# Which engine makes the high parts of q and k, and when q and k are turned: three attention stages of a fused four-layer kernel on one core

## The chip, the core and the metric

One core of a Trainium2 chip runs the whole program. The metric is device microseconds of one execution. The kernel before has a median of 1841.68 us over 3 runs (1833.33 to 1843.39). Engine names as in the profile: PE is TensorE's matmul queue and PEld its weight loads, DVE is VectorE, ACT is ScalarE, POOL is GpSimd, SP is SyncE.

## The reference, cut to what matters

Eight sublayers are added one after another to x, 32 sequences of 128 tokens and 128 features. Three of them are attention with 16 heads of width 8:

```
x = x + L0_xattn(layernorm(x), ctx)         # "cross": biases, output projection
...
x = x + L2_xattn(layernorm(x), ctx, mask)   # "masked": no biases, no output projection
x = x + L2_ffn(layernorm(x))                # begins with causal self attention ("self"):
                                            # rotary q and k, 4 k/v heads, a tanh gate
# in each: softmax(q k^T / sqrt(8)) v, 16 heads
```

The other sublayers (routed experts, attention with one head, attention with 8 heads) aren't touched by the change.

## The kernel before

The function `attention16` writes the three stages, called "cross", "masked" and "self" in its argument `kind`. An item is one sequence (128 tokens on the 128 partitions); there are 32 items. Each engine runs a software pipeline written out by hand: at tick t (`unrolled`), `item(lag)` is item t - lag, and each engine's loop lists which step it does for which lag, in a fixed order. An engine does its list strictly in order, so an instruction that waits on a semaphore holds all that stands behind it on that engine. The tick length is set by the slowest closed loop of such waits.

The lags in cross and masked are F = 1 (project q, k, v), L = 2 (turn, scores), then L + 1 to L + 4; in self F = 2, L = 4, G = 8, O = 9.

Scores are computed twice. Once as they are, to find each row's maximum: q and k are turned by PE (`pe_turn`, L424), k is spread into masked copies `kx` (`v_kx` L709 on DVE in cross and masked, `a_kx` L913 on ACT in self), q is copied to `qT` (`a_qT`, L918, ACT), and PE multiplies them (`pe_scores`, L463; in self preceded by the causal mask, L460). DVE takes the maxima (`v_max`, L717), two halves in a tick. And once transposed, from q and k split in a high part (rounded to fp32r) and a low part, with the maximum as one more column. `high` (L705) writes the high part three times for each head, a cast of 128x768 from a 128x256 source read three times; POOL subtracts it to get the low part (`g_low`, L827). A tick later PE turns these `parts` (`pe_stack_k`, `pe_stack_q`, L430), ACT copies them out (`a_kS` L924, `a_qS` L932, the latter four casts of 32x512), PE multiplies (`pe_scoresT`, L478; in self with a mask matmul, L477), and ACT takes the exponential (`a_exp`, L955), again in two halves.

The next item enters behind that: PE transposes the normalised row (`pe_hT`, L404), ACT copies it out (`a_hT`, L942, or L940 in self), PE projects (`pe_qkv`, L415 and L416, or L412 in self), and DVE takes q, k and v out of PSUM (`v_qkv`, L603 to L619; in self `v_rotate`, L634 to L647). In cross and self the router of the experts that follow is woven in (its transposed rows are copied out by ACT at L2479 or L2477).

Before the change, `high` runs on DVE in cross and masked, behind `v_kx` and `stats`, and on ACT in self, behind `a_kS`. ACT's list in cross and masked is: `a_qT`, `a_qS`, `a_hT`, (route), `a_kS`, `a_exp` twice. DVE's list ends with `v_qkv`, `v_residual`, `v_max` second half, and the next tick begins with `v_kx`. PE's list in self begins with `pe_scoresT` first half, then `pe_turn`, then the router's matmuls, `pe_values`, `pe_stack_k`. `pe_scoresT` waits for the exponential of the half before it, `pe_turn` for the rotated q and k of its item and for the first instruction of `v_rotate` (L634), which frees the PSUM bank that `pe_turn` writes; `pe_stack_k` waits for the residual add of the tick before (L697).

Of the kernel before, what the change touches and what calls it, by code (L numbers as in the profile page):

```python
# [64 lines left out]
def unrolled(last):  # L65

    def tick(t):
        return lambda lag: Item((t - lag) // RING, (t - lag) % RING) if 0 <= t - lag < B else None
    for t in range(B + last):
        yield tick(t)  # L70


def build(nc, a, out):
    ctx = ExitStack()
    with ctx:
# [233 lines left out]
        def attention16(p, before, kind, post=None):  # L309
            at = counted_from(dict(reached))  # L310
            has_bias, masked, causal = kind == "cross", kind == "masked", kind == "self"
# [5 lines left out]
            F = 2 if causal else 1  # L317
            L = 4 if causal else 2
# [10 lines left out]
            s_hi, s_lo = sem("hi"), sem("lo")  # L329
# [194 lines left out]
            def tensor(e):  # L524
                before(e)
                e.wait_ge(s_pad, at(s_pad, n_pad))
                e.wait_ge(sem(p + "weights"), 16 * n_loads[p[:2]])
                e.wait_ge(consts_ready, N_CONSTS)
                if post:
                    e.wait_ge(bf_ready, N_BF)  # L530
                if causal:
                    for item in unrolled(last):
                        if it := item(L + 2):
                            pe_scoresT(e, it, 0)
                        if it := item(L):
                            pe_turn(e, it)
                        if post:
                            pe_post_route(e, item)
                        if it := item(L + 3):
                            pe_values(e, it, 0)  # L540
                        if it := item(L + 1):
                            pe_stack_k(e, it)
                        if it := item(L):
                            pe_scores(e, it, 0)
                        if it := item(L + 1):
                            pe_stack_q(e, it)
                        if it := item(L + 3):
                            pe_values(e, it, 1)
                        if post:
                            pe_post_turn(e, item)  # L550
                        if it := item(F):
                            pe_hT(e, it)
                        if it := item(L):
                            pe_scores(e, it, 1)
                        if it := item(G):
                            pe_gate(e, it)
                        if it := item(L + 2):
                            pe_scoresT(e, it, 1)
                        if it := item(F):
                            pe_qkv(e, it)  # L560
                        if it := item(O):
                            pe_out(e, it)
                else:
                    for item in unrolled(last):
                        if it := item(L):
                            pe_turn(e, it)
                        if it := item(L + 1):
                            pe_stack_k(e, it)
                            pe_stack_q(e, it)
                        if post:  # L570
                            pe_post_route(e, item)
                        if it := item(L + 3):
                            pe_values(e, it, 0)
                        if it := item(L):
                            pe_scores(e, it, 0)
                        if post:
                            pe_post_turn(e, item)
                        if it := item(F):
                            pe_hT(e, it)
                        if it := item(L + 2):  # L580
                            pe_scoresT(e, it, 0)
                        if it := item(L + 3):
                            pe_values(e, it, 1)
                        if it := item(F):
                            pe_qkv(e, it)
                        if it := item(O):
                            pe_out(e, it)
                        if it := item(L):
                            pe_scores(e, it, 1)
                        if it := item(L + 2):  # L590
                            pe_scoresT(e, it, 1)
# [107 lines left out]
            def high(e, it):  # L699
                if due(it.n - RING + 1):  # L700
                    e.wait_ge(s_tq, at(s_tq, it.n - RING + 1))
                e.wait_ge(s_qkf, at(s_qkf, (2 if causal else 1) * (it.n + 1)))
                src = qk[:, it.s % 2].rearrange("p a h d -> p (a h) d").unsqueeze(2).broadcast_to([T, 2 * H16, 3, DH])
                dst = parts[:, it.s, :, :, 0:3, :].rearrange("p a h c d -> p (a h) c d")
                (e.copy if causal else e.tensor_copy)(dst, src).then_inc(s_hi, 1)  # L705

            def v_kx(e, it):
                e.wait_ge(s_turn, at(s_turn, it.n + 1))
# [49 lines left out]
            def vector(e):  # L758
                before(e)
                e.wait_ge(s_pad, at(s_pad, n_pad))  # L760
                e.wait_ge(sem(p + "weights"), 16 * n_loads[p[:2]])
                if post:
                    post["v_start"](e)
                if causal:
                    e.tensor_scalar(w[p + "wo"][:, :], w[p + "wo"][:, :], 0.5, None, ALU.mult).then_inc(s_wo, 1)
                    for item in unrolled(last):
                        if it := item(0):
                            stats(e, it)
                        if it := item(F):
                            v_h2(e, it)  # L770
                        if post:
                            v_post_rows(e, item)
                        if it := item(L):
                            v_max(e, it, 0)
                        if it := item(1):
                            v_y(e, it)
                        if it := item(0):
                            aggregate(e, it)
                        if it := item(L + 3):
                            v_heads(e, it)  # L780
                            v_heads_back(e, it)
                        if it := item(F + 1):
                            v_qk_norm(e, it)
                        if post:
                            post["v_route"](e, item, O)
                        if it := item(L):
                            v_max(e, it, 1)
                        if it := item(F):
                            v_rotate(e, it)
                        if it := item(O):  # L790
                            v_residual_self(e, it)
                        if it := item(G):
                            v_gate(e, it)
                else:
                    for item in unrolled(last):
                        if it := item(L):
                            v_kx(e, it)
                        if it := item(0):
                            stats(e, it)
                        if it := item(F + 1):  # L800
                            high(e, it)
                        if it := item(O):
                            v_heads_back(e, it)
                        if it := item(1):
                            norm(e, it, h[:, it.s, :])
                        if post:
                            v_post_rows(e, item)
                        if it := item(L):
                            v_max(e, it, 0)
                        if it := item(0):  # L810
                            aggregate(e, it)
                        if it := item(L + 3):
                            v_heads(e, it)
                        if post:
                            post["v_route"](e, item, O)
                        if it := item(F):
                            v_qkv(e, it)
                        if it := item(O):
                            v_residual(e, it)
                        if it := item(L):  # L820
                            v_max(e, it, 1)
# [94 lines left out]
            def a_qT(e, it):  # L916
                e.wait_ge(s_kx, at(s_kx, it.n + 1))
                e.copy(qT[:, it.s, :], FR[:, 0:T]).then_inc(s_qT, 1)  # L918
# [40 lines left out]
            def scalar(e):  # L959
# [26 lines left out]
                else:  # L986
                    for item in unrolled(last if post else L + 3):
                        if it := item(L):
                            a_qT(e, it)
                        if it := item(L + 1):  # L990
                            a_qS(e, it)
                        if it := item(F):
# [1807 lines left out]
```

## Time and profile before

| | us |
|---|---|
| median of 3 runs | 1841.68 |
| lowest, highest | 1833.33, 1843.39 |
| the profiled execution | 1839.85 |
| its span in the profile | 1838.0 |
| PE busy | 1493.3 (81%) |
| PE weight loads busy | 1158.7 (63%) |
| DVE busy | 1299.8 (71%) |
| ACT busy | 977.4 (53%) |
| POOL busy | 856.4 (47%) |

The shares are means over stages with different limits. By the first and last starts of the `high` cast, cross runs its 32 ticks with one between 21.2 and 229.5 us, masked between 733.7 and 944.0 us, and self between 981.8 and 1289.4 us. Durations in the profile overlap a little where an engine works without a pause: the next instruction starts before the last one's recorded end. So a tick is best added up from start to start.

### The profile page before, as it was taken

What the parts mean: (1) busy time and instruction counts of PE and PEld (TensorE: products, weight loads), DVE (VectorE), ACT (ScalarE), POOL (GpSimd) and SP (SyncE); (2) the same over time, 40 slices, a digit from 0 to 9 for tenths busy, and PEclk for the clock granted to TensorE, in tenths of its full rate; (3) what the DMA queues carried; (4) which work ended last, traced back from release to release, by engine and by line L of the source; (5) the groups of instructions that cost most, each with busy time, mean ns of one, the idle gap of its engine ahead of it and who ended that gap; (6) DMA issues with size and microseconds to landing.
All of it is one profiled execution on the core that took longest, in us unless ns stands there. A gap on an engine that the chain in (4) does not pass through costs nothing. (4 is left out here: it accounts for less than half of the span.)

```text
span 1838.0 us, 37607 instructions
## 1 busy us (share of the span) xinstructions
PE 1493.3 (81%) x11614; PEld 1158.7 (63%) x11614; DVE 1299.8 (71%) x4152; ACT 977.4 (53%) x2017; POOL 856.4 (47%) x1432
## 2 busy tenths in 40 slices
PE   5999949877998998888876888888676999999830
PEld 3666639865777777555543555555466898888630
DVE  5899942277877776788865788888555688887522
ACT  2888835455433433677763778788443444444310
POOL 2456653374100100233326777898544455665426
PEclk9999969989999999799995999999788899999965
DMA  6786118511000000000000000000075000000043
GB/s 208 238 279 229 39 31 263 169 48 32 1 1 1 1 1 2 7 9 9 9 1 1 1 2 1 6 9 9 21 214 166 14 14 14 21 20 18 12 152 90
DMA packets 60976, 108.56 MB, mean 59 GB/s; under 512 B 11715, under 2 KB 49748, under 8 KB 59988
## 3 DMA queue, kind: packets, MB, share of 16 engines
q1 hardware_dynamic: 54644, 93.67, 16.3%
q0 software_dynamic: 6144, 12.60, 2.3%
q8 instruction: 92, 1.51, 0.3%
q14 instruction: 96, 0.79, 0.1%
HBM read 89.72 MB, written 52.17 MB: 77 GB/s over the span
## 5 line engine op out<-in xcount | busy, mean ns | idle before, releaser
L717 DVE TENSOR_REDUCE parts<-PS 128x8 fp32r<-128x1024 f32 x192 | 234.5, 1221 | 47.6 <-PE PS L463 44.0
L955 ACT ACTIVATE P<-PS 128x1024 f32<-128x1024 f32 x192 | 198.4, 1033 | 72.7 <-PE PS L478 72.6
L932 ACT CAST qS<-PS 32x512 fp32r<-32x512 f32 x384 | 221.2, 576 | 8.6 <-PE PS L430 5.1
L1799 DVE SCALAR_TENSOR_TENSOR X<-PS,wt,X 128x128 f32 (+1 forms) x480 | 134.6, 344 | 47.0 <-PE PS L1642 40.6
L1931 ACT ACTIVATE P<-PS,w_f_b 128x512 f32<-128x512 f32 x128 | 88.0, 688 | 143.4 <-PE PS L1623 141.5
L279 POOL TENSOR_TENSOR ve<-mv,eps_t 128x1 f32<-128x1 f32 x160 | 31.7, 198 | 266.3 <-DVE mv L275 265.9
L1642 PEld LDWEIGHTS PS<-w_f_w,P 128*128 128x128 f32 x1024 | 130.1, 193 | 40.0 <-issue 28.0
L430 PE MATMUL PS<-ident_r,parts 128*128 128x128 f32 x768 | 127.4, 294 | 33.2 <-issue 26.9
L1642 PE MATMUL PS<-w_f_w,P 128*128 128x128 f32 x1024 | 142.1, 283 | 13.9 <-DVE X L1799 12.0
L478 PE MATMUL PS<-qS,kS 128*128 128x512 f32 x384 | 149.7, 445 | 1.1 <-ACT P L955 0.9
L430 PEld LDWEIGHTS PS<-ident_r,parts 128*128 128x128 f32 x768 | 106.2, 201 | 57.4 <-issue 43.8
L846 POOL TENSOR_TENSOR rrs<-rsq,neg_half 128x20 f32<-128x20 f32 x32 | 113.7, 3553 | 43.2 <-DVE rsq L647 43.1
L494 PE MATMUL PS<-P,vx 128*32 128x128 f32 x3072 | 127.8, 287 | 5.0 <-ACT P L955 4.9
L463 PE MATMUL PS<-kx,qT 32*128 32x512 f32 x384 | 101.9, 527 | 2.2 <-ACT qT L918 2.2
L494 PEld LDWEIGHTS PS<-P,vx 128*32 128x32 f32 x3072 | 75.0, 112 | 37.7 <-issue 25.1
L281 POOL TENSOR_TENSOR rstd<-ve,neg_half 128x1 f32<-128x1 f32 x160 | 90.0, 562 | 12.5
L827 POOL TENSOR_TENSOR parts<-qk,parts 128x128 fp32r<-128x128 f32 x192 | 83.9, 457 | 7.7 <-DVE parts L705 6.4
L1455 POOL TENSOR_TENSOR parts<-ident,mx 128x1024 fp32r<-128x1024 f32 x32 | 60.8, 1899 | 54.6 <-DVE mx L1394 54.6
L1854 POOL TENSOR_TENSOR ve<-mv,eps_t 128x4 f32<-128x4 f32 x8 | 1.6, 200 | 180.5 <-DVE mv L1710 180.5
L478 PEld LDWEIGHTS PS<-qS,kS 128*128 128x128 f32 x384 | 66.5, 200 | 21.5 <-ACT P L955 16.5
L1330 PE MATMUL PS<-P 128*128 128x128 f32 x512 | 70.0, 280 | 6.6 <-DVE lgD L2274 3.0
L2439 POOL DMA_INDIRECT hs<-hD,idx x64 | 68.3, 1067 | 13.6 <-issue 12.2
(303 smaller groups left out, 4286.3 us busy)
## 6 DMA issues: line engine op xcount, KB each, us to landing
P<-in_f_blob SPq DMA_DIRECT2D x12, 578.0 KB, 4.7
Y<-in_f_blob SPq DMA_DIRECT2D x11, 578.0 KB, 4.2
ctxT<-in_ctxT SPq DMA_DIRECT2D x128, 48.0 KB, 1.8
tok<-hs SPq DMA_DIRECT2D x46, 128.0 KB, 3.5
hs<-yo SPq DMA_DIRECT2D x46, 128.0 KB, 4.0
P<-in_f_blob SPq DMA_DIRECT2D x12, 450.0 KB, 4.5
Y<-in_f_blob SPq DMA_DIRECT2D x11, 450.0 KB, 4.4
w_f_w<-in_f_w SPq DMA_DIRECT2D x2, 1024.0 KB, 5.6
```

The costliest lines, as they stand in the source:

```text
L281: q.tensor_tensor(rstd[:, it.s, :], ve[:, it.s, :], neg_half[:, 0:1], ALU.pow).then_inc(s_rs, 1)
L430: m = e.matmul(TP[which][:, g * T:(g + 1) * T], parts[:, it.s, which, 4 * g:4 * g + 4, :, :].rearrange("p h c d -> p (h c d)"), ident_r[:, ...
L463: m = e.matmul(S_ps[:, i, :], qT[r:r + 32, it.s, :], kx[r:r + 32, it.s % 2, :, :].rearrange("p j t -> p (j t)"), start=not causal, stop=True)
L478: m = e.matmul(ST_ps[:, i, :], kS[:, it.s % 2, g, :], qS[:, it.s % 2, g, :, :].rearrange("p j t -> p (j t)"), start=not causal, stop=True)
L494: m = e.matmul(OB[32 * g:32 * g + 32, pair * T:(pair + 1) * T], vx[:, it.s, 128 * j + 32 * g:128 * j + 32 * g + 32], P[:, it.s % 2, 4 * g ...
L717: e.tensor_reduce(parts[:, it.s, 0, 8 * half:8 * half + 8, 3, 0], S_ps[:, :, :].rearrange("p i (j t) -> p (i j) t", t=T), AXX, ALU.max)\
L846: e.tensor_tensor(rrs[:, :], rsq[:, :], neg_half[:, 0:n_heads], ALU.pow).then_inc(s_rs3, 1)
L932: m = e.copy(qS[r, it.s % 2, :, j, :], TP[0][r, :].rearrange("p (g t) -> p g t", g=4))
L955: e.activation(P[:, it.s % 2, 8 * half:8 * half + 8, :].rearrange("p h t -> p (h t)"), ST_ps[:, :, :].rearrange("p j n -> p (j n)"), ACT.E ...
L1642: m = e.matmul(YP[(n_steps * b + x) % 2][:, s * T:(s + 1) * T], lhs, w2[:, x, t * D:(t + 1) * D], start=(t == 0), stop=(t == tiles - 1))
L1799: m = e.scalar_tensor_tensor(out=X_s, in0=rows, scalar=wt[:, b, s, x:x + 1], in1=X_s, op0=ALU.mult, op1=ALU.add)
L1931: e.activation(gt[:, (x % 2) * tiles + t, :], ZP[i % 4][:, :], ACT.Gelu if kind == "gelu" else ACT.Relu, bias=b1[:, x, t:t + 1]).then_inc( ...
```

## The change

Three edits. `high` is always `e.copy`, ScalarE's instruction. In cross and masked its call leaves the DVE list and enters the ACT list between `a_qT` and `a_qS`. In self, `pe_turn` goes to the head of PE's list, ahead of `pe_scoresT`. No data, tile or semaphore changes, and no DMA.

```
                 if causal:
                     for item in unrolled(last):
+                        if it := item(L):
+                            pe_turn(e, it)
                         if it := item(L + 2):
                             pe_scoresT(e, it, 0)
-                        if it := item(L):
-                            pe_turn(e, it)
                         if post:
                             pe_post_route(e, item)
...
-                (e.copy if causal else e.tensor_copy)(dst, src).then_inc(s_hi, 1)
+                e.copy(dst, src).then_inc(s_hi, 1)
...
                         if it := item(0):
                             stats(e, it)
-                        if it := item(F + 1):
-                            high(e, it)
                         if it := item(O):
                             v_heads_back(e, it)
...
                         if it := item(L):
                             a_qT(e, it)
+                        if it := item(F + 1):
+                            high(e, it)
                         if it := item(L + 1):
                             a_qS(e, it)
```

## Rows read from the trace of the kernel before

**Rows 1.** Windows: us, engines busy, PEclk, DMA; cross, masked, masked's start, self twice

```profile
184.00:230.00 46.00, 42.66 (x422) 29.96 (x426) 44.30 (x132) 37.07 (x72) 30.47 (x69) 1.00 0.12 37
860.00:900.00 40.00, 34.81 (x344) 22.41 (x336) 34.88 (x86) 31.36 (x55) 12.52 (x36) 1.00 0.03 9
742.00:749.00 7.00, 5.66 (x20) 3.94 (x21) 4.10 (x11) 2.73 (x7) 1.57 (x4) 0.50 0.02 7
1060.00:1080.00 20.00, 18.25 (x113) 12.17 (x114) 15.35 (x49) 14.88 (x33) 15.59 (x26) 0.83 0.01 2
1200.00:1250.00 50.00, 43.16 (x364) 28.65 (x364) 43.93 (x158) 40.63 (x94) 46.45 (x74) 1.00 0.03 8
```

**Rows 2.** Timeline of a masked tick: start us, us, engine, line, [idle before <-releaser]

```profile
857.65 0.27 ACT L918 CAST qT<-PS 128x128 fp32r<-128x128 f32 x1 [0.49 <-DVE kx L709]
857.84 2.34 ACT L932 CAST qS<-PS 32x512 fp32r<-32x512 f32 x4
860.21 0.27 ACT L942 COPY hT<-PS 128x128 f32<-128x128 f32 x1
860.53 0.30 PEld L415 LDWEIGHTS PS<-w_a_wq,hT 128*128 128x128 f32 x2 [0.64 <-ACT hT L942]
861.59 0.35 DVE L606 TENSOR_SCALAR qk<-PS,keep 128x128 f32<-128x128 f32 x1 [0.63 <-POOL parts L827]
862.45 1.22 DVE L717 TENSOR_REDUCE parts<-PS 128x8 fp32r<-128x1024 f32 x1
863.58 0.68 DVE L709 TENSOR_TENSOR kx<-PS,jmask 128x512 fp32r<-128x512 f32 x1
864.30 0.27 ACT L918 CAST qT<-PS 128x128 fp32r<-128x128 f32 x1 [0.49 <-DVE kx L709]
```

**Rows 3.** Timeline of a cross tick

```profile
189.41 0.27 ACT L918 CAST qT<-PS 128x128 fp32r<-128x128 f32 x1 [0.28 <-DVE kx L709]
189.63 2.35 ACT L932 CAST qS<-PS 32x512 fp32r<-32x512 f32 x4
192.48 0.30 PEld L415 LDWEIGHTS PS<-w_a_wq,hT 128*128 128x128 f32 x2 [0.63 <-ACT hT L2479]
196.12 0.27 ACT L918 CAST qT<-PS 128x128 fp32r<-128x128 f32 x1 [0.26 <-DVE kx L709]
```

**Rows 4.** The cast of line 705 by stage (cross, masked, self): ns min/median/max, first and last start

```profile
L705 DVE CAST parts<-qk x32: 542/546/554, 21.2 to 229.5; 128x768 fp32r<-128x768 f32 x32
L705 DVE CAST parts<-qk x32: 542/546/554, 733.7 to 944.0; 128x768 fp32r<-128x768 f32 x32
L705 ACT CAST parts<-qk x32: 834/836/845, 981.8 to 1289.4; 128x768 fp32r<-128x768 f32 x32
```

**Rows 5.** Timeline of ACT in a self tick, around its cast

```profile
1163.05 0.59 ACT L924 CAST kS<-PS 128x512 fp32r<-128x512 f32 x1 [0.75 <-PE PS L430]
1163.54 0.83 ACT L705 CAST parts<-qk 128x768 fp32r<-128x768 f32 x1
1164.27 1.02 ACT L955 ACTIVATE P<-PS 128x1024 f32<-128x1024 f32 x1
```

**Rows 6.** Timeline of masked's second and third tick

```profile
739.80 0.27 ACT L918 CAST qT<-PS 128x128 fp32r<-128x128 f32 x1 [4.33 <-DVE kx L709]
740.44 2.34 ACT L932 CAST qS<-PS 32x512 fp32r<-32x512 f32 x4 [0.38 <-PE PS L430]
747.42 0.27 ACT L918 CAST qT<-PS 128x128 fp32r<-128x128 f32 x1 [3.87 <-DVE kx L709]
```

**Rows 7.** Who waited for the turns in self: us in total, times

```profile
  ACT kx L913: 52.0, 32
```

**Rows 8.** Timeline of the head of the same self tick

```profile
1160.86 1.14 ACT L913 ACTIVATE kx<-PS,jmask 128x128 fp32r<-128x128 f32 x4 [1.27 <-PE PS L424]
1161.94 0.28 DVE L697 TENSOR_TENSOR Y<-Y,PS 128x128 f32<-128x128 f32 x1
1162.33 0.63 PE L430 MATMUL PS<-ident_r,parts 128*128 128x128 f32 x4 [0.81 <-issue]
```

More of the change, by code:

```diff
@@ L532, in tensor @@
                     for item in unrolled(last):
+                        if it := item(L):
+                            pe_turn(e, it)
                         if it := item(L + 2):
                             pe_scoresT(e, it, 0)
-                        if it := item(L):
-                            pe_turn(e, it)
                         if post:
@@ L704, in high @@
                 dst = parts[:, it.s, :, :, 0:3, :].rearrange("p a h c d -> p (a h) c d")
-                (e.copy if causal else e.tensor_copy)(dst, src).then_inc(s_hi, 1)
+                e.copy(dst, src).then_inc(s_hi, 1)
             def v_kx(e, it):
@@ L799, in vector @@
                             stats(e, it)
-                        if it := item(F + 1):
-                            high(e, it)
                         if it := item(O):
@@ L989, in scalar @@
                             a_qT(e, it)
+                        if it := item(F + 1):
+                            high(e, it)
                         if it := item(L + 1):
```

## The prediction

> **What bounds the kernel now.** I read the windows first, to see each touched stage by itself, then the timeline of one steady tick of each, following every start back to what released it. In cross DVE is busy 44.30 of 46 us, PE 42.66, ACT 37.07; in masked PE and DVE are at 34.8 of 40 us and ACT at 31.36 [rows 1]. By these shares DVE looks like the limit of cross, and ACT like the engine with room. The timeline says otherwise. In masked a tick is one closed loop through three engines [rows 2]: ACT copies qT at 857.65, begins qS 0.19 later, and comes to hT at 860.21; PE, which has waited for that copy, starts the projection at 860.53; DVE takes q out at 861.59, does the second maximum at 862.45 and kx at 863.58; and ACT, which has waited for kx, begins the next qT at 864.30. That is 2.56 + 0.32 + 1.06 + 0.86 + 1.13 + 0.72 = 6.65 us, the whole tick. (The wait of DVE at 861.59 is put down to POOL, but L606 reads the PSUM bank that the projection at 860.53 writes, and starts right behind it.) Cross has the same loop: qT 189.41, qS 189.63, PE's wait for the last copy of ACT until 192.48, and qT again at 196.12, 6.71 us [rows 3]. Each of the three engines idles while the other two hold the loop. What matters is so not how busy an engine is but whether an instruction stands inside the loop: on ACT all from qT to hT does; on DVE only v_qkv, the residual, the second maximum and kx do. The DVE cast comes behind kx and ahead of the wait for the projection, outside the loop.
>
> **The change part by part.** *Cast off DVE* (cross, masked). It removes 32 casts of 546 ns a stage [rows 4]. They stand in DVE's time before its wait for the projection, so that wait grows by about as much: nothing gained in a steady tick. Bounds: 0 and 0.55 us a tick; I take 0, since every later start in the loop is released by PE or follows DVE's own work behind that wait [rows 2].
>
> *Cast onto ACT, between qT and qS.* ACT has the same cast in self, 836 ns, in the same shape [rows 4]. From start to start it takes less, since neighbours overlap: 1163.54 to 1164.27, 0.73 us, and kS ahead of it (0.59 long) holds it 0.49, an overlap of 0.10 [rows 5]. So behind a qT of 0.27 the cast starts after 0.17 and qS after 0.17 + 0.73 = 0.90 us. Today qS starts 0.19 (masked) or 0.22 us (cross) after qT [rows 2, 3]. The delay is 0.71 and 0.68 us, 0.70 as a mean, and hT, the projection, the maximum and kx move by it: it stands in the loop and nothing covers it. Its lower bound by rows is 0.68; its upper 0.83, no overlap. The wait that the cast brings to ACT, for q and k of the item, is met: v_qkv wrote them one tick before. Queued behind it are qS, hT, kS and both exponentials, and for hT waits PE. Later than before come POOL's subtraction, by under 1 us, and PE's turn of the parts, which is a tick away, so these don't close a longer loop. PE's output step, which waits for kS, moves with the rest. The tick becomes 7.36 in masked and 7.39 in cross.
>
> Of the 32 ticks with a cast in each stage I count 28 in full: 28 x 0.70 = 19.6 us. The first four run at the lower clock (0.50 in masked's start [rows 1]), and there qS waits for PE and not for ACT: it starts 0.64 after qT, 0.38 of it idle [rows 6], so 0.90 adds only 0.26. Three such ticks make 0.8; the first has no qS yet, and DVE's normalised row comes up to 0.55 earlier there, so about -0.4. A stage: 20.0 us. Two: 40.0.
>
> *Turn at the head of PE's list* (self). ACT waits 52.0 us in 32 ticks for the turns [rows 7], 1.27 in the tick shown [rows 8], and PE could make them about 1.0 us sooner. But the order on ACT goes on with kS, and that waits again, 0.75 us, for PE's L430 [rows 5]; L430 starts after an idle time of 0.81 at 1162.33, which is DVE's residual add of the tick before (1161.94 + 0.28) and its signal [rows 8]. Moving kx up makes the wait of kS longer by the same amount. Nor does the first score product wait for qT in this tick, as its mask matmul follows L430. In the later part of the stage POOL is the limit, 46.45 busy of 50 us [rows 1], and the change takes nothing from it. The cost: scoresT comes behind two transposes and behind L634's release, some 0.3 us later, and the 0.81 of PE's idle time before L430 covers it; without that cover it would be 0.3 x 32 = 10 us. Bounds: -1.0 x 32 = -32 and +10. I take -0.5, for the few ticks at the stage's ends where kS follows qT without a pause; the value is near nothing because two waits in a row have to fall, and only one does.
>
> Sum: 40.0 - 0.5 = +39.5 us. On the profiled execution (span 1838.0, 1839.85 with what lies around it) that is 1879.4; the median of the runs before lies 1.8 above it, so for a median I expect 1881.
>
> **A rule weighed.** In the windows DVE is the fullest vector engine of cross, 96%, and PE 93% [rows 1]. The Trainium skill, Trace Analysis, Identifying the Most-Contended Engine, takes the engine of highest occupancy as the bottleneck and advises working on it first. By it the change helps cross. The loop of rows 3 speaks against that rule here, since ACT at 81% holds a part of the tick that DVE only waits for; its result is the first rival.
>
> **The rivals.** *DVE's fullness is the limit.* If cross were paced by DVE's own work, each of its 32 ticks would lose the cast: -0.55 x 32 = -17.5, masked 0: 1824. For it: 1.7 us of idle in 46. Against it: ACT waits for DVE and PE for ACT inside one tick, which leaves DVE waiting on PE. It decides if PE's projection is done before DVE is ready to take it. Chance 4%.
>
> *ACT's idle time absorbs the cast.* ACT has 8.6 us idle in 40 in masked [rows 1], 1.4 a tick, more than 0.84. If its waits were slack, the stages keep their length: 1841. Against it: the waits stand outside qT to hT. 3%. *Half of it is absorbed*, one stage or half a tick's delay: about 1861. 7%.
>
> *The turn pays.* If kS followed kx up, self would give back up to 32, and half of it is 16: 1865. 4%.
>
> *The clock falls.* PE will wait 0.7 us more a tick, busy about 79% in masked. In self it holds 1.00 at 86%, but a stretch with 18.25 busy of 20 shows 0.83 [rows 1], so the clock can fall from 2.4 to 1.2 GHz for a while inside a steady stage. A tick at the lower level is 7.62 us [rows 6], against 6.65 about 1.0 more. Falling in a third of 56 ticks: +19, 1900. All of them: 1937. 10%, nearly all on the smaller case.
>
> **How the numbers follow.** Forecast 72%, 0.68 to 0.75 a tick: 38 to 42, with ends and self (-3 to +2) and the scatter of a median (some 4 us) 1873 to 1891. The range of 8 in 10 takes in the upper part of the half-absorbed and turn cases and most of the clock case: 1865 to 1896. One measurement tells about 0.5% (9 us) from no change. Faster: the DVE rival and a little of larger gains in self, 5%. Same: absorbed, and part of the half cases, 5%. Slower 90%.
>
> **What would show it.** Right: ACT busy up by 27 us a stage, DVE down by 17.5; the spacing of qT 7.3 to 7.45 us in both stages; qS 0.90 after qT; PE's wait for hT from 0.64 to about 1.3 and DVE's wait for the projection up by 1.2; in self kx earlier by about 1 us, kS's wait for L430 longer by it and ticks of the same length. Wrong: qT spaced as before (the loop is not what I read), a shorter self stage with kS starting right behind qT, or windows of cross and masked with a granted clock under 1.00 behind their start.

## The result, and the profile after

| | before | after |
|---|---|---|
| median, 4 runs each on one chip | 1840.47 | 1875.21 |
| lowest, highest | 1833.33, 1843.39 | 1873.54, 1877.76 |
| span of the profiled execution | 1838.0 | 1874.8 |
| first to last qT of cross, masked | 208.5, 210.5 | 230.4, 229.7 |
| first to last sum of squares in self (L646, one a tick) | 304.3 | 297.8 |

The ratio is 1.0192 (95% interval 1.0172 to 1.0211): slower by 35 us. The median is 6 us under the 1881 forecast. Of the 36.8 us between the two spans cross has 22.0, masked 19.2 and self -6.5. The stretches outside the three stages, which the change doesn't touch, make another 2.1 (+6.0 ahead of masked, +1.9 ahead of self, -5.8 behind self).

The page of the kernel after, its span, busy times and granted clock in 40 slices:

```profile
span 1874.8 us, 37607 instructions
PE 1484.7 (79%) x11614; PEld 1152.8 (61%) x11614; DVE 1272.6 (68%) x4088; ACT 1020.9 (54%) x2081; POOL 855.1 (46%) x1432
PEclk9999977989899999699997899999969899999975
```

ACT has 43.5 us more and DVE 27.2 less than in the table of before. That is less than the 27 and 17.5 a stage of the prediction: from the first to the last qT, ACT has 21.4 more in cross and in masked, DVE 12.8 and 15.7 less; busy time counts the overlap of neighbours only once. By shares only ACT is fuller, 54% for 53%, and the kernel is longer. The windows of the kernel after (same columns as [rows 1]: us, PE, PEld, DVE, ACT, POOL, granted clock, DMA share, GB/s), cross over the same 46 us and masked behind its start:

```profile
184.00:230.00 46.00, 38.30 (x396) 27.48 (x396) 37.71 (x119) 38.00 (x71) 26.65 (x61) 1.00 0.31 108
790.00:980.00 190.00, 147.74 (x1452) 96.20 (x1451) 136.99 (x337) 151.99 (x258) 53.11 (x153) 1.00 0.03 8
```

In cross DVE fell from 44.30 to 37.71, PE from 42.66 to 38.30, and ACT rose by only 0.93, though each tick has 0.83 us more for it: fewer ticks fit into the window. All three are now 82 to 83% busy, and none looks like the limit. The granted clock is 1.00 in both, so nothing was lost to it there.

The timeline of the kernel after, a steady masked tick, from one start of qT to hT and on, and ahead of it DVE's part of the same loop (start, duration, engine, line, [idle before <-releaser]):

```profile
862.39 0.27 ACT L940 COPY hT<-PS 128x128 f32<-128x128 f32 x1
862.71 0.30 PEld L415 LDWEIGHTS PS<-w_a_wq,hT 128*128 128x128 f32 x2 [1.44 <-ACT hT L940]
863.77 0.35 DVE L606 TENSOR_SCALAR qk<-PS,keep 128x128 f32<-128x128 f32 x1 [1.43 <-PE PS L416]
864.63 1.22 DVE L717 TENSOR_REDUCE parts<-PS 128x8 fp32r<-128x1024 f32 x1
865.76 0.68 DVE L709 TENSOR_TENSOR kx<-PS,jmask 128x512 fp32r<-128x512 f32 x1
866.48 0.27 ACT L916 CAST qT<-PS 128x128 fp32r<-128x128 f32 x1 [0.50 <-DVE kx L709]
866.64 0.83 ACT L705 CAST parts<-qk 128x768 fp32r<-128x768 f32 x1
867.37 2.34 ACT L930 CAST qS<-PS 32x512 fp32r<-32x512 f32 x4
869.73 0.27 ACT L940 COPY hT<-PS 128x128 f32<-128x128 f32 x1
```

Beside [rows 2] each link is the same but one: hT to projection 0.32, then 1.06, 0.86, 1.13 and 0.72 as before, and qT to hT 3.25 in place of 2.56. The cast starts 0.16 behind qT and qS 0.73 behind the cast. What ACT takes more, the others wait: PE for hT 1.44 in place of 0.64, DVE for the projection 1.43 in place of 0.63. (The prediction had this wait of DVE up by 1.2; it is up by 0.80, and most of the rest is two new waits earlier in DVE's tick, 0.23 ahead of L288 and 0.26 for PE's scores.) DVE's wait is now put down to PE's L416, where [rows 2] named POOL. The tick is 7.34.

The same in cross, qT to qT 7.39, beside [rows 3]:

```profile
184.75 0.27 ACT L916 CAST qT<-PS 128x128 fp32r<-128x128 f32 x1 [0.26 <-DVE kx L709]
184.92 0.83 ACT L705 CAST parts<-qk 128x768 fp32r<-128x768 f32 x1
185.65 2.34 ACT L930 CAST qS<-PS 32x512 fp32r<-32x512 f32 x4
188.50 0.30 PEld L415 LDWEIGHTS PS<-w_a_wq,hT 128*128 128x128 f32 x2 [1.12 <-ACT hT L2479]
192.14 0.27 ACT L916 CAST qT<-PS 128x128 fp32r<-128x128 f32 x1 [0.29 <-DVE kx L709]
```

The head of a steady self tick of the kernel after, beside [rows 5, 8]:

```profile
1162.36 1.15 ACT L911 ACTIVATE kx<-PS,jmask 128x128 fp32r<-128x128 f32 x4 [0.38 <-PE PS L424]
1164.33 0.28 DVE L697 TENSOR_TENSOR Y<-Y,PS 128x128 f32<-128x128 f32 x1
1164.71 0.64 PE L430 MATMUL PS<-ident_r,parts 128*128 128x128 f32 x4 [0.77 <-issue]
1165.72 0.59 ACT L922 CAST kS<-PS 128x512 fp32r<-128x512 f32 x1 [1.92 <-PE PS L430]
```

The wait of kx fell from 1.27 to 0.38, that of kS rose from 0.75 to 1.92. L430 still starts 0.38 behind the residual add. Such ticks last 10.02 and later 9.73 us in both kernels. The 6.5 us of self are elsewhere. Numbered from the first, its ticks 4 and 5 took 11.51 and 11.13 before and 8.95 and 8.90 after, ticks 10 and 11 11.12 and 10.29 before and 9.90 and 9.91 after; those four make 6.4.

Both pairs lie where the granted clock was low before the change. Windows of the kernel before (new ones), the end of self's start at the lower clock, and the dip (a short fall of the granted clock) behind it:

```profile
1000.00:1020.00 20.00, 18.39 (x84) 11.23 (x83) 11.02 (x36) 14.05 (x28) 13.12 (x19) 0.63 0.00 1
1063.00:1069.00 6.00, 6.00 (x31) 4.09 (x31) 4.38 (x13) 4.01 (x8) 5.27 (x13) 0.50 0.01 3
```

and of the kernel after, whose self begins some 49 us later:

```profile
1029.00:1049.00 20.00, 15.02 (x39) 8.21 (x40) 14.12 (x45) 8.74 (x23) 13.98 (x22) 0.50 0.00 0
1049.00:1069.00 20.00, 17.20 (x119) 10.48 (x119) 15.03 (x48) 15.89 (x32) 15.16 (x21) 0.98 0.01 2
1080.00:1100.00 20.00, 17.75 (x138) 11.23 (x136) 16.71 (x57) 16.19 (x35) 15.11 (x26) 1.00 0.00 1
```

Before, the clock was at 0.50 (1.2 GHz) until 1014, 54 us from self's begin, and again from 1063 to 1069. After, it rose at 1049 to 1050, 41 us from the begin, and it did not fall again in the stage.

### The profile page after: what moved, and what is told of

Same layout as the page of the kernel before. It is cut to its first block and busy times, and to the rows that moved or that the text cites. A ratio compares the mean times of both kernels' runs of the same rounds, so it can differ in the third digit from the quotient of the medians.

```text
span 1874.8 us, 37607 instructions
## 1 busy us (share of the span) xinstructions
PE 1484.7 (79%) x11614; PEld 1152.8 (61%) x11614; DVE 1272.6 (68%) x4088; ACT 1020.9 (54%) x2081; POOL 855.1 (46%) x1432
## 5 line engine op out<-in xcount | busy, mean ns | idle before, releaser
L430 PE MATMUL PS<-ident_r,parts 128*128 128x128 f32 x768 | 129.3, 295 | 32.7 <-issue 30.2
L430 PEld LDWEIGHTS PS<-ident_r,parts 128*128 128x128 f32 x768 | 107.6, 203 | 54.8 <-issue 48.9
L463 PE MATMUL PS<-kx,qT 32*128 32x512 f32 x384 | 101.5, 524 | 2.2 <-ACT qT L916 2.2
L415 PE MATMUL PS<-w_a_wq,hT 128*128 128x128 f32 x128 | 34.3, 353 | 68.0 <-ACT hT L940 43.6
L705 ACT CAST parts<-qk 128x768 fp32r<-128x768 f32 x96 | 80.2, 835 | 0.0
```

The lines of the kernel that those rows point to most:

```text
L430: m = e.matmul(TP[which][:, g * T:(g + 1) * T], parts[:, it.s, which, 4 * g:4 * g + 4, :, :].rearrange("p h c d -> p (h c d)"), ident_r[:, ...
L463: m = e.matmul(S_ps[:, i, :], qT[r:r + 32, it.s, :], kx[r:r + 32, it.s % 2, :, :].rearrange("p j t -> p (j t)"), start=not causal, stop=True)
```

## The experiments

Two theories stood against each other. *Loop:* an instruction costs the time by which it delays qT to hT on ACT (or the links on PE and DVE), and work taken from DVE outside these links is worth nothing. *Fullness:* the busiest engine, DVE in cross, sets the tick. For self: the turn is worth nothing of its own, or it gives what the profile shows.

**Each part alone.** The casts on ScalarE, with PE's order in self as before:

```
                     for item in unrolled(last):
-                        if it := item(L):
-                            pe_turn(e, it)
                         if it := item(L + 2):
                             pe_scoresT(e, it, 0)
+                        if it := item(L):
+                            pe_turn(e, it)
```

> The casts move to ScalarE in cross and masked, between qT and qS, as in the changed kernel; the turn in self stays where it was before. Theory (the loop ScalarE, TensorE, VectorE): tick 7.39 in cross and 7.34 in masked, as in the changed kernel, and self as before the change, so 1840 + 22 + 19 = about 1881 if the 6.5 us that self gave back came from the turn. Rival (self was shorter by the chance of when the clock rose): self shorter here too, about 1875. Rival (VectorE's fullness decides): under 1840, which the changed kernel has all but ruled out.

Measured: 1884.58 (1876.19 to 1886.02), ratio 1.0242 (1.0218 to 1.0266). Cross 231.0 with ticks of 7.38, masked 228.8 with 7.34, self 303.8, ticks 4, 5, 10 and 11 at 10.68, 11.26, 11.15 and 10.28. The casts alone make the whole loss and more. The profiled run was at 1880.17, as expected; the median is 45.5 us above its own before, some 5 more than the span of that profile shows, and the runs without a profile can't say where.

The turn alone (the same lines moved in the kernel before, the cast on DVE):

> Only the turn at the head of TensorE's list in self; the casts stay on VectorE. As predicted before the change: -0.5, about 1840, steady ticks of 9.7 and 10.0 as before and ScalarE's wait for kS longer by what its wait for kx loses. Rival (the turn helps while the clock is low, and lets it rise two ticks earlier): -6, about 1834, with the full clock by some 40 us after the stage's start instead of 54. Rival (the turn pays in each tick): -30.

Measured: 1835.50 (1828.32 to 1839.08, 12 runs), ratio 0.9982 (0.9968 to 0.9995). Masked ticks are 6.65 as before, self is 297.6. So the turn is a small gain in the timed runs too, some 3 us (1 to 6 by the interval), where I had it at half a microsecond.

**Is DVE's time worth anything?** A second cast on DVE in cross and masked (one cast done twice, the result the same):

```
+                if not causal:
+                    e.tensor_copy(dst, src).then_inc(s_first, 1)
+                    e.wait_ge(s_first, at(s_first, it.n + 1))
                 (e.copy if causal else e.tensor_copy)(dst, src)...
```

> The kernel before, with each cast of cross and masked done twice on VectorE, one after the other (some 0.55 to 0.65 us more a tick on that engine). Loop theory: masked's ticks stay at 6.65 within 0.05, since VectorE waits 0.63 for the projection; in cross its wait is only about 0.35, so 0.2 to 0.3 a tick shows; in all 6 to 10 us, about 1848. Rival (VectorE's fullness decides): 0.6 x 64 = 38 us, about 1879.

Measured: 1855.34 (1851.2 to 1862.82), ratio 1.0093 (1.0071 to 1.0115). I had expected masked within 0.05 and 1848 in all: both missed. Masked ticks are 6.80, 0.15 more for 0.56 us of work. DVE's wait for the projection fell from 0.63 to 0.19, so most of the second cast went into it. The small rest has another way: the normalised row now comes late, PE waits 0.93 for it in place of 0.34 and starts the projection 0.46 behind hT in place of 0.32. The wait of PE before the change, and in this kernel:

```profile
858.77 0.14 PEld L404 LDWEIGHTS PS<-ident,h 128*128 128x128 f32 x1 [0.34 <-DVE h L288]
885.40 0.14 PEld L405 LDWEIGHTS PS<-ident,h 128*128 128x128 f32 x1 [0.93 <-DVE h L288]
```

Cross took 18 us more: fourth and fifth tick of 9.49 and 8.39, most later ones of 7.11 to 7.25, and single ones of 9.17, 9.38 and 8.19, each with a fall of the granted clock. Windows with the first two, and one at 1.00 in which DVE is 98% busy, so that its own list probably sets the tick there:

```profile
80.00:120.00 40.00, 37.93 (x351) 25.46 (x350) 38.53 (x109) 32.43 (x61) 18.37 (x52) 0.94 0.75 248
120.00:160.00 40.00, 37.52 (x320) 25.05 (x320) 36.13 (x108) 27.32 (x52) 22.69 (x56) 0.88 0.51 170
190.00:230.00 40.00, 36.87 (x356) 24.26 (x355) 39.12 (x120) 31.39 (x61) 24.11 (x53) 1.00 0.30 103
```

So adding to DVE costs something. Taking from it is another question, and the cast on GpSimd asks it. `high` leaves DVE's list and goes to the head of POOL's tick:

```
                 for item in unrolled(last if post else L + 3):
+                    if it := item(F + 1):
+                        high(e, it)
                     if it := item(0):
                         rsqrt(e, it)
...
```

> The cast of cross and masked on GpSimd, at the head of its tick, where it waits 4.1 us in masked and 2.0 in cross for VectorE's statistics; self as before. From its 128x1024 product (1.9 us) I estimate 1.4 us for the cast. VectorE is so relieved of the cast and ScalarE gets nothing. Loop theory: no change, masked 6.65, 1839 within 4; VectorE's wait for the projection grows by 0.5. Rival (VectorE's fullness decides): -0.5 a tick, -16 in cross alone, 1823. Rival (GpSimd's cast is far slower than I think, over 3 us): both stages longer.

Measured: 1853.84 (1843.81 to 1854.22), ratio 1.0059 (1.0040 to 1.0078), outside the 1839 within 4 that I had expected. The cast on POOL took 829 ns (row of its line, cross and masked), not the 1.4 us of my estimate:

```profile
L705 POOL CAST parts<-qk x64: 822/829/842, 19.5 to 960.5; 128x768 fp32r<-128x768 f32 x64
```

Masked answers the question: neither DVE nor ACT has the cast, and qT is spaced 6.65 to 6.66 us, the tick of before. DVE relieved of 546 ns in each tick gave 0. Cross did not follow: 6.70 from its eighth to about its 19th tick, then mostly 7.05 to 7.22 with single ticks of 9.41 and 9.07, 222.0 in all, 13.5 more than before. The fourth and fifth tick make 4.9 of it (9.49 and 8.25 for 6.31 and 6.52), the late ones the rest. (The profile has no clock record for cross's first ticks and shows 1.00 there. But a matmul of L463 takes 790 ns in them, as in masked's start at 0.50, and 494 ns at 1.00; it does so until 43 us before, until 49 after the change and past 52 us here.) Windows of this kernel, of a stretch that the kernel before spends at 1.00:

```profile
180.00:200.00 20.00, 18.38 (x172) 12.82 (x164) 17.61 (x53) 13.54 (x25) 13.75 (x31) 0.92 0.66 226
200.00:220.00 20.00, 17.93 (x170) 12.20 (x168) 19.43 (x54) 15.43 (x30) 14.53 (x33) 1.00 0.05 16
```

The single long ticks go with clock dips. The 7.05 to 7.22 do not: the slice from 200 to 220 shows them at 1.00 with DVE 97% busy, although it has one cast less. Its rows show what fills it. Here are POOL's issue of the indirect DMA for the experts' rows (L2439) and DVE's scaling L2246 that meets it, and the same line in the kernel before:

```profile
206.43 1.07 POOL L2439 DMA_INDIRECT hs<-hD,idx  x1 [0.18 <-issue]
206.65 1.02 DVE L2246 TENSOR_SCALAR hD<-X,mvD,rsD 128x128 f32<-128x128 f32 x1
190.60 0.39 DVE L2246 TENSOR_SCALAR hD<-X,mvD,rsD 128x128 f32<-128x128 f32 x1
```

From 147 us on, where the long ticks begin, 15 instructions of L2246 and L288 last 0.51 to 1.03 us, for medians of 0.35 and 0.31. Each of them ends within 0.2 us behind the end of an instruction of POOL that overlaps it, mostly L2439 or the cast. In the kernel before no instruction of these two lines lasts over 0.54. Together they are some 8 us longer than their medians. That they set the 7.05 to 7.22 is likely, but no run separates it.

**Where in ACT's list.** The cast one step up, ahead of qT (shown against the casts alone; the turn in self stays as before):

```
+                        if it := item(F + 1):
+                            high(e, it)
                         if it := item(L):
                             a_qT(e, it)
-                        if it := item(F + 1):
-                            high(e, it)
```

> As the casts only, but each cast stands ahead of qT instead of behind it, where ScalarE waits for kx 0.49 us in masked and 0.28 in cross. Loop theory: only what outlasts that wait delays qT. Exp ends its hold at 863.69, the cast takes 0.73, qT at 864.42 instead of 864.30: +0.12 in masked, by the same sum +0.36 in cross: 28 x 0.48 = 13 us, about 1854. Rival (it is the amount of work on ScalarE that counts, not its place): 0.70 a tick, about 1881.

Measured: 1851.64 (1846.35 to 1857.88), ratio 1.0074 (1.0051 to 1.0097). Masked 6.73, cross 6.98. The timeline of a masked tick shows why it is so much cheaper; the cast fills the time in which ACT waited for kx:

```profile
881.26 1.02 ACT L953 ACTIVATE P<-PS 128x1024 f32<-128x1024 f32 x1 [0.89 <-PE PS L478]
882.06 0.68 DVE L709 TENSOR_TENSOR kx<-PS,jmask 128x512 fp32r<-128x512 f32 x1
882.18 0.82 ACT L705 CAST parts<-qk 128x768 fp32r<-128x768 f32 x1
882.90 0.27 ACT L916 CAST qT<-PS 128x128 fp32r<-128x128 f32 x1
```

qT starts 0.84 behind kx's start in place of 0.72 [rows 2]: 0.12 late, as expected, and qS then 0.16 behind qT in place of 0.19. The same instruction on the same engine costs 0.08 us a tick here and 0.69 one place later. In cross, where the wait for kx is shorter, it costs 0.29 (6.98 for 6.69), somewhat under the expected 0.36.

Between the two exponentials, where ACT waits 0.88 for PE in each tick:

> The cast of cross and masked on ScalarE between the two exponentials, where that engine waits 0.89 us for the scores; self as before. It leaves the stretch from qT to hT, so nothing of the loop that goes through hT. But POOL's subtraction now starts behind it, at about 862.65 instead of 861.04 in the masked tick, its end at 863.5 releases the turn of the parts 0.9 us later than now, and qS, which follows that turn, starts some 0.4 us later. Loop theory: a second loop becomes the longer one, +0.4 a tick in masked, +0.6 in cross: 28 x 1.0 = 28, about 1867, and the wait that ends last is TensorE's L430 for POOL's parts. Rival (only what stands between qT and hT counts): 1839.

Measured: 1869.11 (1867.93 to 1869.64), ratio 1.0153 (1.0137 to 1.0169). Masked 6.97, cross mostly 7.14, with two ticks of 8.56 and 8.52. The place is outside qT to hT, and costs 0.32 us in masked all the same. Its timeline shows another chain:

```profile
880.70 0.84 ACT L705 CAST parts<-qk 128x768 fp32r<-128x768 f32 x1
881.62 0.87 POOL L825 TENSOR_TENSOR parts<-qk,parts 128x128 fp32r<-128x128 f32 x2 [1.62 <-ACT parts L705]
882.54 1.11 PE L430 MATMUL PS<-ident_r,parts 128*128 128x128 f32 x8 [0.71 <-POOL parts L825]
883.74 2.34 ACT L930 CAST qS<-PS 32x512 fp32r<-32x512 f32 x4 [0.24 <-PE PS L430]
```

Late parts make PE's turn late, and that holds qS back to 0.51 behind qT, where [rows 2] has 0.19: that is the 0.32. A cast has two neighbours, the list it stands in and the one who reads it.

**A version built on the loop.** If the loop is qT to hT, the way to shorten it is to bring hT forward. The turn at the head, the cast on DVE, and hT (and the route's copy) ahead of the last quarter of qS:

```
-            def a_qS(e, it):
+            def a_qS(e, it, js=range(4)):
...
-                            a_qS(e, it)
+                            a_qS(e, it, range(0, 3))
                         # a_hT, route
+                            a_qS(e, it, range(3, 4))
                         # a_kS, a_exp twice
```

> The turn at the head in self (as the turn only), casts on VectorE; and in cross and masked ScalarE copies hT (and the router's row) ahead of the last quarter of qS instead of behind all of it: 0.58 us out of the loop, nothing added or left out. Loop theory: TensorE is busy with the values until 860.15 in the masked tick, so the projection starts 0.37 earlier: tick 6.28, -10. In cross the turns of the parts and VectorE (6.45 busy a tick) are close behind: -0.1 to -0.25 a tick, -3 to -7. With the turn's -4: about 1820. Rival (the loop is not what sets the tick; the changed kernel was slower because ScalarE got more work): as the turn only, about 1835.

Measured: 1817.57 (1814.83 to 1818.79), ratio 0.9868 (0.9852 to 0.9885): it beats both kernels. Masked ticks are 6.21, cross 6.50 to 6.70, self 300.7. The timeline of a masked tick:

```profile
851.25 0.30 PEld L415 LDWEIGHTS PS<-w_a_wq,hT 128*128 128x128 f32 x2 [0.20 <-ACT hT L943]
852.31 0.35 DVE L606 TENSOR_SCALAR qk<-PS,keep 128x128 f32<-128x128 f32 x1 [0.19 <-PE PS L416]
855.02 0.27 ACT L918 CAST qT<-PS 128x128 fp32r<-128x128 f32 x1
855.22 1.76 ACT L932 CAST qS<-PS 32x512 fp32r<-32x512 f32 x3
856.99 0.27 ACT L943 COPY hT<-PS 128x128 f32<-128x128 f32 x1
857.28 0.58 ACT L932 CAST qS<-PS 32x512 fp32r<-32x512 f32 x1
```

qT to hT is 1.97 in place of 2.56. The waits for hT and for the projection shrank to 0.20 and 0.19, and the tick gained 0.44 of the 0.59. ACT now starts qT without a pause, so a second loop is the next limit: ACT's own list, with the 0.88 us in which it waits between the two exponentials for PE's scores. Masked is 14.0 us shorter than before (196.5), cross 2.1 (206.4; its fourth tick took 8.95 in place of 6.31) and self 3.6. The turn is part of this kernel, so not all of the 1.3% comes from hT.

The same with the cast on POOL, to see whether DVE holds anything once the loop is shorter:

> The one before with the cast of cross and masked on GpSimd. Loop theory: with the loop through hT shorter, VectorE's work of 6.45 a tick and its row for TensorE are the next limit of cross, so here the relief counts: up to 0.2 a tick beyond the one before in cross, 0 to 0.2 in masked: about 1814. Rival: GpSimd's later subtraction holds TensorE's turn of the parts: slower than the one before.

Measured: 1828.53 (1825.66 to 1830.48), ratio 0.9930 (0.9917 to 0.9943), 11 us slower than the version just above, not faster as I expected, and as the rival had it. Masked 6.20, no gain; its fourth and fifth ticks 9.48 and 7.17 for 8.31 and 6.21. Cross 210.4 for 206.4, again good first and then 6.6 to 7.4, with L2248 and L288 (the same two steps of DVE) at up to 0.99 us as above. One tick of 9.40 lies in this window:

```profile
180.00:200.00 20.00, 19.15 (x175) 13.39 (x175) 17.27 (x47) 14.34 (x29) 13.60 (x29) 0.83 0.23 74
```

**Self once more.** Is the turn's gain the order's, or the clock's? The kernel before and the turn alone, each profiled again, and the cast ahead of qT with the turn:

> The kernel before once more, for one profile. Open is why self took 6.5 us less with the turn at the head (303.8 to 304.3 us from its first to its last row reduction with the old order, 297.6 to 297.8 with the new one). Theory: the program's own order decides when TensorE is granted its full clock in self's start, so the same program gives the same stage: 303.9 within 0.5, with ticks 4 and 5 at about 11 us and 10 and 11 at about 11 and 10.3. Rival: when the clock rises and dips differs from execution to execution, and the old order falls on 297 to 304 by chance: then this one may be at 298 or 301.

Measured (one run): 1833.69, self 300.0, not 303.9. Ticks 4 and 5 took 10.24 and 9.87, ticks 10 and 11 9.91 and 9.92: the same program, and this time no fall of the clock behind 1060. The window in which [rows 1] shows 0.83, in this execution:

```profile
1060.00:1080.00 20.00, 16.83 (x137) 11.05 (x135) 17.04 (x54) 15.74 (x36) 15.81 (x27) 1.00 0.01 2
```

> The kernel before with the turn at the head alone, once more, for one profile. Theory: self again 297.7 us within 0.5, with ticks 4 and 5 at 9.0 and 8.9. Rival (the clock differs from execution to execution): anything from 297 to 304.

Measured (one run): 1832.86, self 297.3, ticks 4 and 5 at 8.95 and 8.90.

> The cast on ScalarE, put ahead of the copy of qT instead of behind it in cross and masked, and the turn at the head in self. Theory: the ticks are those of the same cast without the turn, 6.73 us in masked and 6.98 in cross, and self is 297.7 us in place of 301.4, so 1851.6 - 3.7 = 1848 us. Rival: the turn is worth nothing of its own and the 301.4 stays, 1852; or the clock decides and self is anywhere from 297 to 304 (1847 to 1854).

Measured: 1846.02 (1843.35 to 1847.79), ratio 1.0031 (1.0018 to 1.0044). Masked 6.72 to 6.73, cross 6.98, self 297.7, as the first theory had it.

So over all profiles self took 300.0 to 304.3 with the old order (seven, mean 303.0) and 297.3 to 301.1 with the turn at the head (six, mean 298.7). The ends overlap, and one program moved by 4.3 from one execution to another. The mean gain is 4.3. Timed, the turn is worth a ratio of 0.9982 by itself; with its cast between qT and qS the ratios 1.0192 and 1.0242, with its cast ahead of qT 1.0031 and 1.0074 differ by 0.4 to 0.5%, 8 to 9 us; in both pairs the two were timed on different occasions.

The clock in the same 13 profiles splits them more sharply than the lengths do. Count from self's first L646. With the old order the clock falls again in all seven once it has risen: in six it rises at 26 to 27 us, falls about 3.4 us later and stays at 0.50 for 3.4 or 10 us; the seventh rises at 41. In five of the seven there is a fall of 6.8 us at 88, in another one at 136. With the turn at the head it rises at 27 us (four) or 37 (two), and falls in none of the six before the stage ends. The stretch right behind the rise and the next one in the kernel before, profiled again, then the stretch behind the rise with the turn alone, profiled again:

```profile
1001.10:1004.50 3.40, 2.03 (x10) 1.23 (x11) 1.42 (x2) 3.36 (x8) 3.40 (x2) 1.00 0.02 5
1005.00:1008.00 3.00, 3.00 (x9) 1.81 (x8) 1.90 (x4) 1.52 (x3) 2.69 (x8) 0.51 0.00 0
1004.50:1007.90 3.40, 2.81 (x16) 1.64 (x15) 2.00 (x5) 3.02 (x5) 3.40 (x3) 1.00 0.02 5
```

Behind the rise PE is busy for 59 to 70% of the time in the six profiles with the old order that rise at 26 to 27, and then the clock falls; it is busy for 82 to 83% in the four with the turn at the head that rise there, and the clock stays. So the order does act on the clock. That PE's pauses are what brings the fall is likely by these rows, but no run separates it.

## Why the prediction was right, and where it was off

*What bounds the kernel.* Right. In masked the links of the loop kept their lengths to 0.01 us when one was stretched, and the loop, with the one through POOL and PE beside it, priced the cast in masked at three places of ACT's list (0.69 a tick for 0.70 between qT and qS; 0.08 for an expected 0.12 ahead of qT; 0.32 for 0.4 between the exponentials) and hT brought forward (6.21 for 6.28).

*Cast off DVE: 0.* Right, shown in masked by the cast on POOL: 6.65 with 0.55 us less on DVE. The reason also held in the rows: the wait ahead of L606 grew, to 0.74 there and to 1.43 in the changed kernel. In cross that kernel can't clear the rival "DVE's fullness", as its late cross ticks were longer. Two others speak against it: it wanted 17.5 us less with the change, and cross became 22.0 longer; and with hT brought forward cross's ticks fell from 6.69 to between 6.50 and 6.70 with DVE's work as it was. With a second cast DVE seems to become the limit of late cross (98% busy), so the engine was not far from it.

The rule that picks the engine of highest occupancy (the Trainium skill, Trace Analysis, Identifying the Most-Contended Engine) is contradicted by these traces: in masked DVE has the highest share (34.88 of 40 us, PE 34.81), and relieving it of 0.55 us a tick left the tick at 6.65, while moving one copy on ACT (31.36 of 40), with no work taken from any engine, made it 6.21.

*Cast onto ACT: 0.70 a tick, 20.0 a stage.* Right: ticks 7.34 and 7.38 to 7.39 for 7.36 and 7.39. Stages 19.2 and 22.0. In masked that is 27 ticks in full and not 28, with 0.24 and 0.28 in the second and third and nothing in the first and fourth. Cross is 2.0 over, and that is its fourth tick: 8.89 us for 6.31 before, a difference of 2.58, in which L463 still takes 790 ns as at the lower clock. Other kernels with untouched early ticks have anything from 6.29 to 9.49 there, so I don't lay it to the cast. The two stages together: 41.2 for 40.0.

*ACT's idle time absorbs it*, in full or half: refuted in this order. But it was not a wrong thought, only the wrong place: ahead of qT it absorbs nearly all of it in masked (0.08 of 0.73 is left) and more than half in cross (0.29).

*Turn: -0.5.* This is the term that was mis-sized: -6.5 between the two profiles, -4.3 as a mean over all, about -3 to -9 in timed runs. The step said that two waits in a row have to fall and only one does. That is what the steady tick shows (0.38 and 1.92 for 1.27 and 0.75, length the same). Its remark that POOL limits the later part rests on POOL's share alone and was not tested. The step failed where it priced the stage by its steady ticks. The difference sits in four ticks while the granted clock is low or falls, and there I had put nothing. That the order acts on the clock is shown by six profiles without a fall behind the rise against seven with one. How large the effect is in one execution stays loose, as the same program had these two ticks at 11.51 and 11.13 once and at 10.24 and 9.87 the next time.

*The clock falls*, as a rival for cross and masked: did not happen (1.00 in both windows), and the clock moved the other way in self.

*The sum.* 39.5 forecast, +1.2 in cross and masked, -6.0 in self and +2.1 outside the three stages give the 36.8 of the two profiles; the medians lie 34.7 apart.

## What to carry to other kernels

Before moving work to an engine with room, write down one steady tick as a loop, start by start, and see whether the new instruction stands between the signal that the engine receives and the one that others wait for; the same 0.83 us cost 0.69, 0.32 or 0.08 us a tick in masked by its place in the list. Then look for the reader of what it makes, which is a second loop. The same reading tells what to bring forward: one copy ahead of a quarter of another took 0.44 us off each masked tick where the change added 0.69. Then look for what the shorter loop exposes, and when the granted clock is low, compare it in several profiles, as it can be worth more than the steady tick.

## What the hardware showed that I had not expected

GpSimd made the 128x768 cast from fp32 to fp32r in 829 ns, as fast as ScalarE (836 ns), where VectorE takes 546 ns. Its price was no reason against it; what speaks against it is that cross got longer with the cast there both times, by 13.5 and by 4.0 us.

VectorE was held up by GpSimd in cross: with the cast on GpSimd a 128x128 scaling of VectorE took up to 1.03 us in place of 0.35, and each long one ended within 0.2 us behind the end of a GpSimd instruction. So VectorE, relieved of a cast, still stood at 97% of 20 us there, where it had 96% of 46 before.

The granted clock of one program differs from execution to execution: the kernel before had 0.83 in the window 1060 to 1080 in one profile and 1.00 in another, and self took 304.3 and 300.0 us. A gain of a few microseconds that lies in such ticks needs several profiles before it is put down to an edit. Whether the clock fell behind its first rise in self went with PE's order in all 13 profiles, seven against six.

Inside cross four kernels (the double cast, the cast between the exponentials, both with the cast on POOL) had windows of 0.83 to 0.94 and single ticks of 8.2 to 9.4 us. PE's busy share in these windows, 92 to 96%, says little, since the same matmul takes longer at the lower clock (790 ns for 494 of L463 in masked). The fastest version, with PE at 54.71 of 60 us, has none there:

```profile
180.00:240.00 60.00, 54.71 (x539) 36.72 (x537) 54.84 (x170) 50.12 (x90) 38.69 (x86) 1.00 0.13 41
```

What else sets the dips apart stays open.
